# Sums and transposed maxima beside the products with V, a narrow unit's last three products in one group, and a selection ahead of both additions

## The reference

```python
qkv = x @ W_attn + b_attn                     # 16 heads of 32
scores = einsum('bhki,bhqi->bhkq', k, q) / sqrt(32), masked where key > query
attn = softmax(scores over k);  combined = attn.T @ v
x = layernorm(x + combined @ W_out + b_out)
# top half of the tokens by x @ w_router, through an FFN of 2048 (gelu), weighted by sigmoid(score)
x = layernorm(x with the update added at the chosen tokens)
```

## Time and profile before

| | us |
|---|---|
| median of 3 runs | 2603.3 (2601.86 to 2606.7) |
| profiled execution | 2603.97 |
| its span, first to last instruction | 2602.2 |
| PE busy | 2507.7 (96%) |
| POOL busy | 1600.0 (61%) |
| DVE busy | 1665.0 (64%) |
| ACT busy | 1234.6 (47%) |

### The profile page before, as it was taken

The page is one execution under the profiler, slowest core; times in us unless marked ns, Lnnn a source line. Parts: engine busy times, 40 slices in busy tenths (PEclk is TensorE's granted clock), DMA queues, the critical chain, the costliest instruction groups (busy, mean ns, idle before and its releaser), DMA issues.

```text
span 2602.2 us, 40583 instructions
## 1 busy us (share of the span) xinstructions
PE 2507.7 (96%) x13920; PEld 1821.6 (70%) x13920; DVE 1665.0 (64%) x4231; ACT 1234.6 (47%) x2354; POOL 1600.0 (61%) x1666
## 2 busy tenths in 40 slices
PE   7899999999999999999999999998999999999998
PEld 5565666667666667666667666674588888888886
DVE  6666667667767767777676677667465535544533
ACT  2555566566665666665666565665631111111110
POOL 1676788887888787888787888887241213122211
PEclk8998999999999999999999999998999999999999
DMA  7556567676666866657676576764430101011010
GB/s 144 91 97 129 115 151 167 127 152 145 139 143 126 171 141 137 155 130 141 127 181 126 119 175 127 142 130 131 155 106 33 33 25 41 17 30 36 17 33 17
DMA packets 167263, 286.46 MB, mean 110 GB/s; under 512 B 23121, under 2 KB 58001, under 8 KB 165906
## 3 DMA queue, kind: packets, MB, share of 16 engines
q1 hardware_dynamic: 159890, 267.01, 47.6%
q0 software_dynamic: 7168, 16.85, 2.0%
HBM read 116.97 MB, written 65.11 MB: 70 GB/s over the span
## 4 chain that ended last, share of the span: by engine, by line
PE 55%; POOL 34%; ACT 4%; issue 3%; DVE 2%; DMA 1%; SPq 0%; POOLq 0%; ACTq 0%; DVEq 0%
POOL Pa L786 29%; PE PS L1467 13%; PE PS L1446 13%; PE PS L1324 6%; PE PS L1412 5%; PE PS L1396 5%; PE PS L1365 4%; PE PS L1316 4%; PE PS L1330 2%; POOL Pm L763 2%; PE PS L1339 1%; POOL P L763 1%; ACT Pm L909 1%; DMA Kp<-nat 1%; POOL lnrs L799 1%
## 5 line engine op out<-in xcount | busy, mean ns | idle before, releaser
L786 POOL TENSOR_TENSOR Pa<-Pa,Pm 128x512 f32<-128x512 f32 (+1 forms) x623 | 770.9, 1258 | 153.7 <-ACT Pm L909 96.4
L1396 PE MATMUL PS<-Qp,Kp 98*128 98x512 f32 (+3 forms) x1536 | 550.9, 363 | 31.5 <-ACT Pm L909 13.1
L909 ACT ACTIVATE Pm<-PS 128x512 f32<-128x512 f32 (+3 forms) x856 | 395.4, 471 | 294.4 <-PE PS L1396 240.3
L1365 PE MATMUL PS<-Kp,Qp 96*128 96x512 f32 (+3 forms) x1536 | 500.6, 362 | 14.9 <-DMA Kp<-nat 5.1
L1006 DVE TENSOR_REDUCE nm<-PS 128x1 f32<-128x512 f32 x512 | 344.4, 685 | 193.2 <-PE PS L1365 192.5
L1396 PEld LDWEIGHTS PS<-Qp,Kp 98*128 98x128 f32 x1536 | 292.2, 192 | 241.8 <-ACT Pm L909 119.6
L786 POOL TENSOR_TENSOR Pa<-Pa,P 128x512 f32<-128x512 f32 (+1 forms) x307 | 381.8, 1263 | 73.3 <-ACT P L909 46.2
L876 ACT ACTIVATE G<-PS,b1c 128x512 f32<-128x512 f32 x128 | 88.2, 689 | 539.6 <-PE PS L1446 539.6
L1014 DVE CUSTOM_DVE_ANT_0 PS<-PS,maskA,nm 128x384 f32<-128x384 f32 (+3 forms) x512 | 263.3, 554 | 116.0 <-PE PS L1365 112.4
L1014 DVE CUSTOM_DVE_ANT_0 PS<-PS,maskA 128x384 f32<-128x384 f32 (+3 forms) x512 | 245.0, 506 | 137.9 <-PE PS L1365 137.9
L1365 PEld LDWEIGHTS PS<-Kp,Qp 96*128 96x128 f32 x1536 | 284.9, 195 | 68.4 <-DVE nm L1014 9.9
(11 more groups left out here) (142 smaller groups left out, 4261.9 us busy)
## 6 DMA issues: line engine op xcount, KB each, us to landing
Qp<-nat SPq DMA_DIRECT2D x192, 256.0 KB, 6.8
Kp<-nat SPq DMA_DIRECT2D x192, 256.0 KB, 5.7
o_s<-Of SPq DMA_DIRECT2D x64, 256.0 KB, 2.1
Ot<-o_s SPq DMA_DIRECT2D x64, 256.0 KB
xb<-in_x SPq DMA_DIRECT2D x64, 256.0 KB, 3.3
h_s<-hs SPq DMA_DIRECT2D x64, 256.0 KB, 3.4
out<-xb SPq DMA_DIRECT2D x64, 256.0 KB, 3.5
x_raw<-in_xt SPq DMA_DIRECT2D x15, 1024.0 KB, 6.4
```

The costliest lines, as they stand in the source:

```text
L786: e.tensor_tensor(to, to, probs(u, k)[:, h0:h0 + many, 0:w], ALU.add).then_inc(s["padd"], many)
L909: e.activation(probs(u, k)[:, h_, 0:w], PS[:, B_BANKS[j % 2], 0:w], ACT.Exp).then_inc(s["b_exp"], 1)
L1365: ins = e.matmul(to, Qp[0:96, u % 4, h_, qt * P:qt * P + P], Kp[0:96, (2 * i + k0 // 512) % 4, h_, 0:w], start=True, stop=True)
L1396: e.matmul(PS[:, B_BANKS[j % 2], 0:w], Kp[0:98, (2 * i + k // 4) % 4, h_, k % 4 * P:k % 4 * P + P], Qp[0:98, u % 4, h_, 512 - w:512], star ...
```

## The change

F of the even unit moves from beat 10 to the very end of beat 15, F of the odd one from place 31.6 to 31.99. N may start at beat 15 of its slot in both units (before: 10 and 14, where other jobs had ended), so it stands at beats 15 and 31, behind F. Products: e0 one beat after its step is formed instead of three, which is beat 31, behind F and N of the period before; e1, e2 and e3 in one group two beats after e3 is formed, beat 6; the odd unit's as before. On POOL the last selection of a unit (step 3 or 7) goes ahead of the first of the two additions of the step before it; it stood between them.

```diff
-F_LAG = (1.6, 1.6)
+F_AT = (15.99, 31.99)
...
-PRODUCTS = (((0,), (1,), (2, 3)), ((0,), (1, 2), (3, 4), (5, 6, 7)))
+PRODUCTS = (((0,), (1, 2, 3)), ((0,), (1, 2), (3, 4), (5, 6, 7)))
+PV_LAG = ((1, 2), (2, 2, 3, 3))
...
             return 13 if job[1] % 2 else 8
-        return 14 if job[1] % 2 else 10
+        return 15
...
-            ring.append((u // 2 * 2 * BEATS + end + F_LAG[u % 2], ("F", u)))
+            ring.append((u // 2 * 2 * BEATS + F_AT[u % 2], ("F", u)))
...
-                k1 = max([g for g in PRODUCTS[u % 2] if k in g][0])
-                n = self.formed[u, k1] + (2 if diag(u, k1) is None else 3)
+                j, k1 = [(j, max(g)) for j, g in enumerate(PRODUCTS[u % 2]) if k in g][0]
+                n = self.formed[u, k1] + PV_LAG[u % 2][j]
...
-                            if h0 == 2 and kept_early(u, k + 1):
+                            if h0 == (0 if k + 2 == ksteps(u) else 2) and kept_early(u, k + 1):
                                 keep(u, k + 1)
```

## The result

The kernel after the change takes 2574.0 us (median of 4 runs, 2573.1 to 2576.3) where the kernel before, timed beside it, takes 2604.8 (4 runs, 2601.9 to 2606.7): ratio 0.9885, 95% interval 0.987 to 0.990, a gain of 30.7 us. Forecast were 2560 and a gain of 44; the time lies inside the range.

The account below looks back on a forecast made before the run. The period was taken to close through POOL's 33.5 us run and PE's way from the sums on; 1.27 us a period, 37.5 in all, plus 6.8 of clock, taken from 2603.3, gave 2560 us; eight in ten from 2548 to 2582.

Parts of the forecast that it names:

- e0: Product of the even unit's step 0, behind the odd sums on PE: POOL's selection for it ready with 0.2 us margin.
- port clashes: Rival, chance 0.15: one more POOL clash with VectorE's two-input operation in every period's long run, costing 12.4 us: 2572.
- no change: Rival, chance 0.04: the last product's stall moves whole to odd sums and e0, joins turn into waits: 2603.
- the slower kernel: Rival, chance 0.05: PE stands at the new group for e0's selection, and half clock follows: 2715.
- joins and position alone: Rival, chance 0.15: ACT or a tile's exponential waits elsewhere, no clock comes back, 23 us remain: 2580.
- Step 1: Groups on PE: nine become six, each join worth 0.22 us; two lie after POOL's run: 0.44 a period.
- step 3: Odd unit's sums: one tile and F later, 0.31 us; start 0.05 instead of 0.27 behind POOL's addition, 0.22.
- Step 4: ACT's logarithm and exponential run while PE is at e0, so the score tile's stall goes: 0.30 us.
- Step 6: PE's arrival at odd sums: 962.8, waiting 0.3 us for POOL; e0's selection is done with a margin of 0.2.
- Step 2: F beside products: bounds a gain of 0.14 us and a loss of 0.22 us; taken as 0.
- Step 5: Last selection ahead of both additions: the last product's 0.62 us wait goes, POOL's end stays at 963.04.
- The clock: Early periods: four half-clock stretches, half taken to go as the last product's stall splits: 6.8 us, bounds 0 and 13.6.

Follow-up runs that it names:

- experiment 6: Changed kernel with the product of the even unit's step 1 a group of its own again, at beat 3: 2578.1 us, ratio 0.991.
- Experiment 7: Changed kernel with ACT's two normalising copies of an output tile two beats later: 2587.8 us, ratio 0.995.
- experiment 3: Changed kernel with both F at their old beats, 2577.4 us; then the even F there, the odd F ahead of the even unit's waiting score tile, 2571.6 us.
- experiments 1 and 2: First: changed kernel with the last selection back between the additions, 2600.7 us. Second: kernel before with only that selection moved ahead of both, 2597.0 us.

## Why the prediction was right or wrong

**The sign, the range and the mechanism** were right: PE's way behind POOL's unbroken run was shortened, POOL's run stayed at 33.5, the sums came up to it, and the last product's wait went. The rivals of port clashes, of no change and of the slower kernel did not come: POOL lost no time, e0 found its selection done 0.38 ahead, against a margin of 0.2 forecast (0.28 by its own numbers, since 963.04 + 0.63 is 963.67). Of the rival of joins and position alone one half came, waits of PE elsewhere.

**The sum was too high**, 1.27 for 0.87 to 0.92. The period splits in three: from the odd sums to POOL's first addition 20.34 us instead of 21.00 (889.76 to 910.10, before 908.54 to 929.54), POOL's run 33.45 instead of 33.50, and from its end to the sums 0.10 instead of 0.27:

```profile
889.76 1.06 PE L1342 MATMUL PS<-Pa,ones 128*32 128x512 f32 x8
```

Within the first, 0.66 less, positions and waits are read from the rows, and the joins have what is left:

| step of the prediction | forecast | measured |
|---|---|---|
| 1, two joins behind the sums | 0.44 | 0.54 |
| 3, sums one tile and F later | 0.31 | 0.07 |
| 3, sums closer to POOL's end | 0.22 | 0.17 |
| 4, the wait of 0.30 goes | 0.30 | 0.05 |
| 5, POOL's run unchanged | 0 | 0.05 |

- *Step 1.* A join is worth 0.33 (0.32 in experiment 6) and not 0.22. For two that is 0.22 more; but 0.11 of it, the slower start of the matmul behind the sums (909.54 to 909.82), was read as a cost of F and stands in step 3's 0.31. So the text was 0.1 too low here.
- *Step 3, position.* Tile e1.1 (0.17) and F went ahead of the sums as forecast. But the sums' own due time moved as well, and a piece of the V projection (two matmuls of 256 columns, 0.23), that stood behind tile o1.3 now stands ahead of it: between the sums and that tile there were 21 such pieces and are 22. The step follows what the change moves, and not what the planner moves in its stead.
- *Step 4.* The 0.30 at e1.3 went as said, but 0.25 came at e3.0, some 4 us behind the sums (949.65 to 950.37, for two matmuls that take 0.47), behind the copies at 948.54 and 949.25. The text looked at the next tile only ("ACT is late there by nothing that I see"), and not at those after it. Experiment 7 shows this wait moving and growing, not going.
- *Step 6.* PE was to be there 0.3 ahead of POOL. It comes at the same time, 0.10 behind POOL's end and so 0.05 late. What was not counted is above all the wait of 0.44 at e1.1, whose cover (the sums between e1.0 and e1.1) the change takes away, and that PE waits 0.40 at the tiles of o7 instead of 0.32; the piece of V gone from this stretch and the larger join took a part of it back. The text asked what covers the sums, not what the sums cover.
- *Step 2* was right. F beside products was taken to cost what it costs alone. The group F, sums, o1, o2 lies between the plain matmuls at 916.03 and 919.18 (below): less 0.23 it takes 2.92 us, against 1.08 + 1.94 - 0.22 = 2.80: 0.12. Beside the odd sums it is 0.11 (experiment 3). Alone it is 0.11 too: before, the even F starts at 928.67, the next matmul at 928.70 and the one behind that at 929.01, 0.03 and 0.08 more than the 0.23 of a full matmul; the 0.11 ahead of it that the text read from 909.54 to 909.82 comes from the sums, and the even F, behind a plain matmul (928.44), has none. The Trainium skill, TensorEngine Tiling (Array Packing), section Key Properties, has the engine drain when the tiling mode changes; the runs agree for products (0.33 for a group of one's own), and F costs a third of that, beside products or not. Timeline of PE after:

```profile
916.03 0.39 PE L1368 MATMUL PS<-Kp,Qp 96*128 96x512 f32 x1
916.26 0.27 PE L1375 MATMUL PS<-identf,nm 128*16 128x128 f32 x1
916.46 1.07 PE L1342 MATMUL PS<-Pa,ones 128*32 128x512 f32 x8
917.35 1.90 PE L1415 MATMUL PS<-Pm,V 128*32 128x512 f32 x16
919.18 0.50 PE L1399 MATMUL PS<-Qp,Kp 98*128 98x512 f32 x1
```

- *Step 5.* Right in its 0.62 and that POOL's end would not move. What the step did not see is how much hangs on it: alone 0.22, in the company of the rest 0.80 (experiments 1 and 2). The terms are not independent: they lie on one path, and the sum holds only if all are there.
- *The clock.* The early gain came out at the 6.8 taken, 13.6 us less of 34 at half clock, but by luck: the text counted four stretches where there were five, and its reason, the stall that splits, doesn't carry it. With the selection alone the stall splits as well, and the time at half clock stays 34 us; with the selection back it is 34 too, in the kernel after 20, with e1 apart 10. In the kernel of the selection alone 10.2 us at half clock follow the two parts:

```profile
118.87 0.43 PE L1412 MATMUL PS<-Pm,V 128*32 128x128 f32 x8 [1.09 <-POOL Pm L763]
...
122.69 1.94 PE L1339 MATMUL PS<-Pa,ones 128*32 128x512 f32 x8 [1.60 <-POOL Pa L786]
```

And 5 us were lost from beat 992 on, as PE was at half clock for 10 us more there; for this stretch the text had a gain of 0.2.

By stretches: to beat 288 forecast 3.0 + 5 x 1.27 + 6.8 = 16.2, measured 11.8; 22 periods more 27.9, measured 21.6; the end of attention +0.2, measured -3.8. The differences, 4.4 + 6.3 + 4.0, are the 14.7 that the gain falls short of 44.3 by in the profiled execution.

**Open**: why more of the tail is at half clock. From beat 1019 to the feed-forward's first matmul it takes 57.3 us before and 56.8 with the selection alone, but 60.9 in the kernel after and 58.2 and more in all the other kernels run. So it seems to come with the joins or the moved sums, and not with the selection; no run tells these apart. Open too is what sets the early time at half clock, which moves from kernel to kernel between 10 and 38 us.

## What to carry to other kernels

When an operation is moved, list both what it waits for and what it was covering: two score tiles with two banks need 1.1 us between them, and the sums that stood there were that time. When two engines close a loop, a gain on one shows only up to the other, so terms on one path are tested together and apart; here 0.22 and less than 0.1 made 0.9. A group's cost is read to the second matmul behind it, and not to the first: 0.33 and not 0.22 here. And where a planner sets the order, read the new order for what was swapped in.

## What the runs showed of the hardware

- F, a transposition of 16 columns, costs 0.12 and 0.11 us of PE in a group of column-tiled matmuls, and 0.11 between full ones.
- A group of eight column-tiled matmuls between full ones costs 0.33 us for being apart; 0.11 of it falls on the first full matmul behind it (0.34 to the next start instead of 0.23). The first matmul behind a wait is as slow (0.28 instead of 0.17 at 943.17).
- Stalls of 1.08, 0.45 and 0.99 us in one early period end come with 3.4 us at half clock, where one of 2.35 and a smaller one came with 6.8; a period later 10.2 us at half clock (173.6 to 184: granted 0.51) begin behind stalls of 0.72 and 0.45, and a third of 0.88 lies inside. With the selection alone, stalls of 1.09 and 1.60 came with 10.2. Splitting a stall is no sure way to keep the clock. Timeline of PE after, the first of these:

```profile
118.30 0.42 PE L1415 MATMUL PS<-Pm,V 128*32 128x128 f32 x8 [1.08 <-POOL Pm L766]
120.85 0.27 PE L1375 MATMUL PS<-identf,nm 128*16 128x128 f32 x1
122.11 1.73 PE L1342 MATMUL PS<-Pa,ones 128*32 128x512 f32 x8 [0.99 <-POOL Pa L789]
```

- The clash of POOL with VectorE's two-input operation stayed single: in the kernel before it hits a selection (1.09 for 0.63), after it an addition (1.46 for 1.0), with POOL's run equally long.
